# Masks, expert weights and set-up of a graph layer with mixture of experts dealt out anew, and a part of the adjacency loaded from ScalarE's queue

## What is computed

```python
mask = (adj > 0)
agg = mask @ norm(x) / max(mask.sum(1), 1)
combined = concat([norm(x) @ W_self + b_self, agg @ W_nb + b_nb])
x = x + relu(combined @ W_comb + b_comb)
logits = norm(x) @ Wg + bg                      # (4096, 8)
w, e = softmax(top2(logits)), the two experts
x = x + sum over the two of w * (gelu(norm(x) @ W1[e] + b1[e]) @ W2[e] + b2[e])
```

## Time and profile before

| | us |
|---|---|
| median of 3 runs | 525.07 (524.85 to 525.54) |
| span of the profiled execution | 521.0 |
| PE busy | 444.2 (85%) |
| DVE busy | 370.7 (71%) |
| POOL busy | 305.2 (59%) |
| ACT busy | 257.6 (49%) |

### The profile page before, as it was taken

How to read it: one execution, slowest core, us unless ns; L and a number is a source line. 1 busy time by engine, 2 the same in 40 slices (tenths; PEclk the granted TensorE clock), 3 DMA queues, 4 the chain that set the end, 5 groups by cost and what they waited for, 6 DMA issues and landing times.

```text
span 521.0 us, 12708 instructions
## 1 busy us (share of the span) xinstructions
PE 444.2 (85%) x4162; PEld 380.2 (73%) x4162; DVE 370.7 (71%) x1056; ACT 257.6 (49%) x403; POOL 305.2 (59%) x346
## 2 busy tenths in 40 slices
PE   4599989999999999989799899745999999997720
PEld 3388878888888888768688688633887778876610
DVE  2889744858758888679587798662677777679982
ACT  2558660543634354344354342330677777776630
POOL 2679778244355766756567563676255556555570
PEclk9789999999999999989999899965799999999975
DMA  8999898599999999999999931964555555588665
GB/s 247 267 264 270 239 243 221 147 278 258 256 272 277 298 306 307 299 297 276 301 282 307 291 132 62 275 230 153 166 164 164 164 161 153 149 325 335 195 211 161
DMA packets 49167, 122.47 MB, mean 235 GB/s; under 512 B 11081, under 2 KB 20173, under 8 KB 48080
## 3 DMA queue, kind: packets, MB, share of 16 engines
q1 hardware_dynamic: 31632, 68.29, 47.2%
q0 software_dynamic: 16080, 50.49, 32.4%
q10 hardware_dynamic: 1392, 2.88, 1.9%
HBM read 96.52 MB, written 26.93 MB: 237 GB/s over the span
## 4 chain that ended last, share of the span: by engine, by line
PE 27%; DVE 21%; DMA 19%; issue 12%; ACT 6%; SPq 6%; POOL 5%; another core or an unknown queue 2%; DVEq 1%; ACTq 0%; POOLq 0%
DMA wst<-in_L_ffn_W_dram 11%; PE bank L1326 7%; PE bank L1346 7%; PE bank L1227 6%; SPq L440 5%; POOL stage L563 3%; DMA x_sb<-in_x_dram 2%; DMA stage<-in_adj_dram 2%; PE bank L1218 2%; PE bank L1219 2%; DMA stage<-in_adj_dram,gidx 2%; PE bank L1313 2%; DVE stage L1112 2%; DVE mask L820 2%
## 5 line engine op out<-in xcount | busy, mean ns | idle before, releaser
L1218 PE MATMUL bank<-z_flat,maskT 128*128 128x257 f16 x1024 | 231.6, 277 | 0.7 <-issue 0.4
L1219 PE MATMUL bank<-z_lo,maskT 128*128 128x256 f16 x1024 | 231.5, 276 | 0.0
L642 POOL DMA_INDIRECT pair_out<-rows,enum x78 | 79.6, 1021 | 66.9 <-DVE gate L1125 29.7
L563 POOL DMA_INDIRECT stage<-in_adj_dram,gidx x64 | 76.0, 1188 | 64.3 <-ACT mask L667 52.0
L1218 PEld LDWEIGHTS bank<-z_flat,maskT 128*128 128x128 fp8e4 x1024 | 101.4, 99 | 14.2 <-issue 0.5
L1219 PEld LDWEIGHTS bank<-z_lo,maskT 128*128 128x128 fp8e4 x1024 | 101.4, 99 | 13.0 <-issue 0.3
L574 POOL DMA_INDIRECT dispatched<-rows,slot x64 | 65.9, 1030 | 39.5 <-issue 20.2
L710 ACT ACTIVATE xh<-x_sb,nb,rs 128x256 f32<-128x256 f32 x32 | 19.2, 600 | 139.6 <-POOL nb L631 139.6
L667 ACT ACTIVATE mask<-stage,m 128x2048 fp8e4<-128x2048 int32 x32 | 64.0, 2001 | 15.2 <-DVE maskT L827 7.5
L1346 PE MATMUL bank<-w,stage 128*128 x468 | 60.7, 281 | 8.2 <-DVE stage L1112 4.3
L1326 PE MATMUL bank<-stage,w 128*128 128x256 f16 x468 | 61.4, 284 | 6.2 <-DVE stage L1098 4.4
(11 more groups left out here) (175 smaller groups left out, 586.0 us busy)
## 6 DMA issues: line engine op xcount, KB each, us to landing
stage<-in_adj_dram SPq DMA_DIRECT2D x256, 128.0 KB
stage<-dispatched SPq DMA_DIRECT2D x39, 260.0 KB
wst<-in_L_ffn_W_dram SPq DMA_DIRECT2D x16, 256.0 KB
z_lo<-pair_out SPq DMA_DIRECT2D x4, 1024.0 KB
dispatched<-pad SPq DMA_DIRECT2D x15, 260.0 KB
out_dram<-x_sb SPq DMA_DIRECT2D x28, 128.0 KB
maskT<-pair_out SPq DMA_DIRECT2D x3, 1024.0 KB, 8.5
x_sb<-in_x_dram ACTq DMA_DIRECT2D x6, 256.0 KB, 8.5
```

What stands on the lines that cost most here:

```text
L563: gp.indirect_dma_start(out=stage[:, s, b - 2, :], out_offset=None, in_=adj_q[:, :], in_offset=bass.IndirectOffsetOnAxis(ap=gidx[:, 0:1], ...
L642: gp.indirect_dma_start(out=yp_dram[:, :], out_offset=bass.IndirectOffsetOnAxis(ap=enum[:, a, s:s + 1], axis=0), in_=ysb[:, a, s, :], in_o ...
L1218: mm(acc[u % 2][:, 0:D + 1], a, z_hi[:, i, :], start=(i == 0), stop=False)
L1219: last = mm(acc[u % 2][:, 0:D], a, z_lo[:, i, :], start=False, stop=(i == NT - 1))
```

## The change

- The pairs phase makes five masks (tiles 0 to 4, after pairs 1, 4, 7, 10, 13). Which tile's mask is made in a main step is told by `made_in`: tile 5 in step 0, tile t + 3 in steps 3 to 9, t + 2 in 11 to 15, t + 1 in 17 to 30, none in the others. The transposition (`turned_in`) is of tile t + 1 in steps 3 to 16 and of tile t from 18 on, and stands behind L902. GpSimd's gather of two tiles later follows `made_in`.
- From tile 8 on (`SHARED`) SP issues row quarters 0 and 1 of the direct half (four transfers of 128 KB); ScalarE issues quarters 2 and 3, two transfers of 256 KB, at the end of its step, behind its mask and behind a wait for DVE's mask of the same tile (`load_adj` in ScalarE's program). `landed(t)` gives the semaphore's count, 96 instead of 128 for such a tile.
- ScalarE also issues the expert weights: expert 0 after the pairs, expert k + 1 at the end of step 4k + 5, behind a wait for DVE's expert_lo of expert k.
- L1252 stands behind the whole product, not between its halves.
- Set-up: statistics of groups 1 and 2, the normalising of tiles 4 to 7, the split of the gate's weights and the z transposes of pairs 2 to 4 move behind the first products' needs; TensorE's first pair waits for the folded weights only. `zt_behind` says which z transposes follow a pair.
- GpSimd's self_and_const(1), (2) come before gather(6), and gather(7) moves to the main steps.

The diff, cut to its core:

```diff
...
+        def zt_behind(i):
+            return [j for j in {0: (2, 3), 1: (4,), 2: (5, 6), 3: (7, 8)}.get(i, (i + AHEAD,)) if j < PAIRS]
...
-        MASKS, HELD, MADE = (1, 3, 6, 8, 10, 12), 4, 2
+        MASKS, HELD = (1, 4, 7, 10, 13), 4
+        def made_in(s):
+            if s == 0:
+                return len(MASKS)
+            for first, end, ahead in ((3, 10, 3), (11, 16, 2), (17, NT - 1, 1)):
+                if first <= s < end:
+                    return s + ahead
+            return None
+        SHARED = made_in(3) + 2
+        def landed(t):
+            first = [i for i in range(t % 2, t + 1, 2) if i < SHARED]
+            return 128 * len(first) + 96 * (t // 2 + 1 - len(first))
+        def turned_in(s):
+            if 3 <= s <= 16:
+                return s + 1
+            return s if 18 <= s < NT else None
...
-                    for g in (0, 2, 1, 3):
+                    for g in (0, 2, 1, 3) if t < SHARED else (0, 1):
-            def load_expert(k):
-                if k:
-                    sp.wait_ge(s_el, 2 * k)
-                for w, m in enumerate((W1, W2)):
-                    sp.dma_start(wst[:, w], m[k].rearrange("(t p) n -> p t n", p=P)).then_inc(s_ew, 16)
...
-                if t == len(MASKS):
-                    load_expert(0)
-                if t >= B + HELD + 1 and t % B == 1:
-                    load_expert((t - HELD - 1) // B)
-            load_expert(E - 1)
...
-            self_and_const(0)
+            for k in range(3):
+                self_and_const(k)
-            self_and_const(1)
-            self_and_const(2)
-            gather(7)
...
-                if HELD <= s < NT - 2 - MADE:
-                    gather(s + 2 + MADE)
+                m = made_in(s)
+                if m is not None and m + 2 < NT:
+                    gather(m + 2)
-                for _ in range(1 if s < NT - 2 - MADE else 2):
+                for _ in range(1 if s < NT - B else 2):
...
+            def load_adj(t):
+                s = 2 * (t % 2)
+                act.wait_ge(s_mD, t - 1)
+                for g in (2, 3):
+                    act.dma_start(stage[Q * g:Q * g + Q, s, :, :], adj_v[t // B, t % B, g, :, 0:2, :]).then_inc(s_adj[s], 16)
...
+            def load_expert(k):
+                if k:
+                    act.wait_ge(s_el, 2 * k)
+                for w, m in enumerate((W1, W2)):
+                    act.dma_start(wst[:, w], m[k].rearrange("(t p) n -> p t n", p=P)).then_inc(s_ew, 16)
-            for k in range(OWN // B):
-                normalise(k)
-            for i in range(AHEAD - 1):
-                zt_hi(i)
+            normalise(0)
+            zt_hi(0)
+            zt_hi(1)
-            zt_hi(AHEAD - 1)
+            normalise(1)
-                if i + AHEAD < PAIRS:
-                    zt_hi(i + AHEAD)
+                for j in zt_behind(i):
+                    zt_hi(j)
+            load_expert(0)
...
-                if HELD <= known < NT - MADE:
-                    masks(t + MADE, u + MADE, known + MADE)
+                m = made_in(t)
+                if m is not None:
+                    masks(m, m, m)
+                    if SHARED <= m + 2 < NT:
+                        load_adj(m + 2)
+                if t >= ESPLIT and (t - ESPLIT) % B == 0 and (t - ESPLIT) // B < E - 1:
+                    load_expert((t - ESPLIT) // B + 1)
...
-                dve.wait_ge(s_adj[s], 128 * (div(t, u, known, 0, 2) + 1))
+                dve.wait_ge(s_adj[s], landed(t))
...
-            stats(1)
-            stats(2)
+            stats(1)
...
-            v.tensor_scalar(wg_s[:, 0], wg_f[:, :, :], scw[:, 1:2], None, ALU.mult).then_inc(s_wf, 1)
-            dve.wait_ge(s_wf, 1)
-            v.scalar_tensor_tensor(wg_s[:, 1], wg_f[:, :, :], scw[:, 1:2], wg_s[:, 0], ALU.mult, ALU.subtract).then_inc(s_wf, 1)
+            stats(2)
+            v.tensor_scalar(wg_s[:, 0], wg_f[:, :, :], scw[:, 1:2], None, ALU.mult).then_inc(s_wf, 1)
+            dve.wait_ge(s_wf, KT + 1)
+            v.scalar_tensor_tensor(wg_s[:, 1], wg_f[:, :, :], scw[:, 1:2], wg_s[:, 0], ALU.mult, ALU.subtract).then_inc(s_wf, 1)
-            for i in range(2, AHEAD):
-                zt_lo(i)
...
-                if i + AHEAD < PAIRS:
-                    zt_lo(i + AHEAD)
+                for j in zt_behind(i):
+                    zt_lo(j)
...
-                if HELD <= known < NT:
-                    mask_transpose(t, u, known)
+                m = turned_in(t)
+                if m is not None:
+                    mask_transpose(m, m, m)
...
-                if HELD <= known < NT - MADE:
-                    masks(t + MADE, u + MADE, known + MADE)
+                m = made_in(t)
+                if m is not None:
+                    masks(m, m, m)
...
-            for i in range(3):
-                z_transpose(i)
+            z_transpose(0)
+            z_transpose(1)
-            for i in range(3, AHEAD):
-                z_transpose(i)
...
+                    neighbours(u, 1, known == 0).then_inc(s_mm, 1)
-                if live(known, 0):
-                    neighbours(u, 1, known == 0).then_inc(s_mm, 1)
...
-            pe.wait_ge(s_wf, KT + 2)
+            pe.wait_ge(s_wf, KT)
...
-                if i + AHEAD < PAIRS:
-                    z_transpose(i + AHEAD)
+                for j in zt_behind(i):
+                    z_transpose(j)
+            pe.wait_ge(s_wf, KT + 2)
```

## The result

The changed kernel takes **546.44 us** (median of five: 541.09 to 548.64). The kernel before took 525.07 beside it (524.20 to 528.06). The ratio is **1.039, 95% interval 1.033 to 1.045: slower**, where 513 and faster was forecast. On another chip, later, it was 1.039 again (1.034 to 1.044). The profiled execution took 541.09 us, with a span of 539.3; the forecast of the span was 508.8, so 30.5 us have to be explained. It was the fastest of the five, 5.4 us under the median, and its device time is 1.8 us more than its span; the 4.1 us that the prediction put between span and median were in part such a difference between executions. A ratio is of the means of those runs that lie within 1.5% of the fastest of their kernel, so it can differ by some thousandths from the ratio of the medians.

The account below looks back on a forecast made before the run. The loop between engines and nearly full DMA were taken to bound the kernel. Span 521.0 - 335.0 + 322.8 (last product's end) = 508.8; median 525.07 - 12.2 = 512.9, said as 513; range 502 to 523 (the sum's own 506 to 519).

Parts of the forecast that it names:

- step 10, to tile 13: Step 10 makes no mask but its chain still runs 6.2 us; with 7.6, tile 13's mask comes at 146.3.
- step 16, to tile 18: Step 16, also empty, costs another 13.8 us from tile 17's mask at 179.1 to tile 18's at 192.9.
- Set-up: Before the pairs: reordered work starts the first pair near 20.3, 4.0 us earlier, and the first product at 74.4.
- The pairs themselves keep their pace: Between set-up and first product: the pairs run as before, so the 4.0 us won reach the first product.
- Product 0 ended at 85.5 and ends at 81.5 now, so SP's load of tile 8 goes out at about 85.: Start of the main steps: tile 8's load goes out at about 85 instead of 96.3, filling the DMA hole.
- my first rival: Head start kept: tile 31 some 9 us earlier than in the sum, span 504; against it, full DMA; chance 0.14.
- Rounds of 8.9: Steps 3 to 9: transposition ahead of ScalarE's mask lengthens the round by 1.3 to 8.9 us; tile 12 at 132.5.
- Late rounds of 8.2: Steps 11 to 30: rounds of 8.2 us, between 7.95 and 8.38, as some of DVE's 10.8 us weight wait goes.
- The heart of the sum: Tile 31's mask at 299.5 in step 30, against 302.1 in step 29: hardly earlier, but fewer products left behind it.
- ScalarE's loads at 0: ScalarE's two issues a step, 0.93 us, fit its idle time, so cost 0; above, 1.9 us a step.
- The starved gathers: Rival: with two direct queues the gather gets a third instead of half, costing 5 to 12 us; 519; chance 0.11.
- My one rival on the slower side: ScalarE becomes the bound: issues of 1.0 us add 0.8 us to 24 steps, 19 us, so 532; chance 0.08.

Follow-up runs that it names:

- d_setup: The kernel before with the new set-up only; masks, loads and steps as before; ratio to before 1.008.
- k_order: h_abm with X1 of tile 0 ahead of tile 6's mask, and GpSimd's second and third additions held until tile 4's mask is made; ratio to before 0.988.
- a_spread: The changed kernel with GpSimd's addition for group 3 held until tile 5's mask, those of groups 4 to 7 dealt out to steps 4 to 7; ratio to before 1.036.
- b_tr_first: The changed kernel with DVE's transposition of a mask ahead of the subtraction in every step; ratio to before 1.016.
- l_mask_first: The changed kernel with DVE's mask ahead of X1, nothing else; ratio to before 1.026.
- n_tr_early: The changed kernel with DVE's transposition ahead of the subtraction in steps 3 to 16 only; ratio to before 1.020.
- e_unsplit: The kernel before with the small matmul that needs an expert's maximum behind the whole product, not between its halves; ratio to before 1.003.
- c_sp_all: The changed kernel with all quarters issued by SP again, expert weights still from ScalarE; ratio to before 1.037.
- m_order_sp: k_order with all the direct loads from SP's queue again; ratio to before 0.987.
- r_after: The changed kernel again, unedited, beside others on another chip; ratio to before 1.039.
- h_abm: The changed kernel with GpSimd's additions dealt out to the steps, DVE's transposition ahead of the subtraction, and DVE's mask ahead of X1; ratio to before 0.982.
- q_order2: h_abm with X1 of tile 0 ahead of tile 6's mask, GpSimd's first three additions in one go as in the change; ratio to before 0.987.
- i_before_m: The kernel before with DVE's mask ahead of X1 instead of behind it; ratio to before 0.997.
- b: The edit of b_tr_first: DVE's transposition ahead of the subtraction; alone on the changed kernel, ratio to before 1.016.
- m: The edit that puts DVE's mask ahead of X1; alone on the changed kernel it is l_mask_first, ratio to before 1.026.
- a: The edit of a_spread: GpSimd's additions dealt out to the steps; alone on the changed kernel, ratio to before 1.036.

## Why the prediction was wrong

By its own steps, the 30.5 us between the forecast span and the measured one:

| step | forecast | measured | miss, us |
|---|---|---|---|
| first product | 74.4 | 75.7 | 1.3 |
| X1 of tile 0, from the first product | 7.1 | 18.2 | 11.1 |
| to ScalarE's mask of tile 7 | 6.5 | 8.9 | 2.4 |
| five rounds, to tile 12 | 44.5 | 47.4 | 2.9 |
| step 10, to tile 13 | 13.8 | 14.3 | 0.5 |
| to tile 17 | 32.8 | 33.7 | 0.9 |
| step 16, to tile 18 | 13.8 | 15.3 | 1.5 |
| 13 rounds, to tile 31 | 106.6 | 110.4 | 3.8 |
| to the last product's end | 23.3 | 26.0 | 2.7 |
| after it | 186.0 | 189.4 | 3.4 |

**Set-up: right in place, worth nothing.** The first pair is at 20.26 where 20.3 was said. "The pairs themselves keep their pace" failed: 1.3 us short here, and all of it gone in d_setup, where a mask held by GpSimd's additions stands among the pairs.

**Masks: the step that failed first.** "Product 0 ended at 85.5 and ends at 81.5 now, so SP's load of tile 8 goes out at about 85." The load went out at 97.6. I moved DVE's mask of tile 5 into step 0 and did not look at what GpSimd does there. The row that told it was in the trace of the kernel before, GpSimd's and DVE's timelines at 77 to 89 us:

```profile
77.07 11.60 POOL L593 TENSOR_TENSOR rows<-rows,const_bc 128x1024 f32<-128x1024 f32 x5
```

```profile
86.58 2.38 DVE L914 SCALAR_TENSOR_TENSOR x_sb<-xh,x_sb 128x256 f32<-128x256 f32 x1
```

An addition of X1 that takes 0.43 us elsewhere took 2.38 and ended at 88.96, 0.29 us after the five additions (88.67). The Trainium skill (SBUF - State Buffer, SBUF: two separate sides) says why: GpSimd and DVE share a pair of ports as "an **exclusive lock**, not a bandwidth split", taken by a DVE operation in a mode that uses both ports, or with two SBUF inputs. No run shows the mask's mode other than by these stalls. The rule fits the traces: the loser stands still (end of the train plus 1.1 us for a mask, plus 0.29 for X1's addition). They show more: it stands still over five GpSimd instructions in a row, 11.6 us, not over one. k_order shows it by the length of the train: one addition instead of three, 1.58 us instead of 6.19.

Two more things were wrong in that sentence. From step 3 on the transposition of tile t + 1 stands ahead of X1, so already X1 of tile 0 has 1.2 us in front of it that I left out (84.13 in a_spread, 92.72 in the changed kernel). And with the stall gone the mask of tile 6 waited for data until 90.97 in a_spread, so 85 was out of reach there too; this is what my first rival's "against" had said, data asked for sooner need not come sooner. Of the 8.6 us that a_spread wins back at X1 of tile 0, 3.7 are left at ScalarE's mask of tile 7 (99.1 against 102.8) and 4.4 at the last product.

**Rounds of 8.9: the size failed.** The 1.3 us for the transposition were right (2.79 us from normalising to mask, 2.8 forecast), and b_tr_first shows their cost. Missing was 0.6 us a round: the gather's first DMA, which began just ahead of DVE's mask before and took 1.47 us, now begins just behind it and takes 2.06 (1.26 in l_mask_first, where the mask is over by then). The same page of the Trainium skill (Who interferes with whom) has this too: such a DMA of GpSimd's own queue waits for descriptors, which GpSimd can't write while DVE holds the ports. The trace agrees: the DMA ends at 126.10, 0.90 us after the mask (125.20), and the second one, with no mask beside it, takes 0.95.

**Late rounds of 8.2: wrong by 0.3.** I priced the transposition's place in steps 3 to 9 and at nothing in steps 18 to 30, where it stands behind the subtraction as well. With it ahead of the subtraction b_tr_first has 8.1; n_tr_early against b_tr_first points to the late steps' own share, but one execution of each does not settle it. The loads' part of the claim was right in itself: DVE's wait for weights fell from 10.8 to 2.1 us, but the rounds did not follow.

**"The heart of the sum" was not one.** "The last mask is hardly earlier, but fewer products are left behind it": 26.0 us are left behind it, where 32.9 were before and 23.3 were forecast. But tile 31's mask is made in step 30, not 29, and a step more ahead of it is worth a round only if the steps keep their pace; the mask came at 323.9, not 299.5. Nor does the undivided product have a share in it: e_unsplit has 33.0 us left and a ratio of 1.003. The 9.9 us that TensorE waited inside products were slack of a loop that was late anyway.

**ScalarE's loads at 0: right** (c_sp_all, m_order_sp; 0.85 us for two in the trace). The starved gathers did not appear: ScalarE's masks wait for gathered data 0.6 us, as before. The Trainium skill's rule (DMA: Bandwidth & Descriptors, Rules for kernel authors) that another issuing engine gives no bandwidth held: with SP alone the ratio is 1.037 against 1.039, and 0.987 against 0.988. My one rival on the slower side, ScalarE as the bound, had the wrong engine: ScalarE's idle time was ended by GpSimd's nb (138.5 us), and what lengthened that chain was between DVE and GpSimd.

**The end.** 189.4 us against 186.0; before-like kernels had 187.1 (d_setup) to 190.8 (e_unsplit). r_after has 170.6 us there, beside 167.1 to 167.8 in the other three on its chip. Whether 3 us are the change's was not tried further.

**Was the scheme good?** With the three orders mended, the ratio is near the forecast's: 0.982 (0.974 to 0.991) in h_abm, 0.987 in q_order2, against 513/525 = 0.977. That does not show that the scheme earns it. i_before_m has nothing of the scheme, only DVE's mask ahead of X1, and ends its last product at 328.8, as the mended versions do, with 500.54 us beside k_order's 498.83. What the scheme adds to that one edit is not told from nothing here. The order is worth the whole of the difference between 4% slower and 1 to 2% faster: b 0.023 and m 0.013 alone, a 0.003 alone (not told from nothing), all three 0.057. Together they give more than their sum (0.039); b alone, for one, only hands the train's stall on to X1. If a part of the scheme carries some of it, it is not the set-up, the loads' queue or the undivided product alone, by d_setup, m_order_sp and e_unsplit. The three mended versions with ScalarE's loads (h_abm, k_order, q_order2) end their last product within 1.4 us of each other, at X1 of tile 0 from 85.3 to 90.2; what sets that end, now that the start doesn't, is open.

## What to carry to other kernels

Before an instruction is moved, look at what every other engine does at the place it moves to, not only at what it waits for: a DVE instruction that GpSimd's work holds up (a mask, an addition of X1) is a wait that no semaphore shows. An instruction far over its usual duration in the old trace is the place to look. Look also whether the data of an instruction that is moved ahead is there by then. In a loop across engines, price the order within the step in every step that has it, and do not count waits of an engine outside the loop as gain.

## What the runs showed that was not expected

- DVE instructions can be held over a whole train of GpSimd additions: 6.19 and 13.03 us for 1.2, and 2.38, 7.21 and 7.77 us for 0.43, each ending 1.1 us (a mask) or 0.28 to 0.29 us (an addition) after the train.
- The part after the last product depends on the chip. The kernel before took 524 and 527 us on two chips and 505 and 506 on two others. It was profiled on one chip only, but the changed kernel was on two: 189.4 us after its last product in one, 170.6 in the other (r_after), while up to that product the second was not faster (349.9 and 355.2). Windows over that part, of the kernel before and of i_before_m on one of the faster chips:

```profile
335.00:521.00 186.00, 137.43 (x1297) 111.63 (x1294) 125.89 (x322) 106.08 (x204) 97.81 (x98) 0.87 0.62 196
```

```profile
328.80:497.00 168.20, 129.60 (x1297) 112.00 (x1294) 125.56 (x327) 108.56 (x204) 104.35 (x99) 0.90 0.68 217
```

The same number of matmuls, with 217 instead of 196 GB/s. So only ratios, not microseconds, are compared across chips here.
